# One softmax kernel, one core: 5 of every 64 exponentials move from ScalarE to VectorE

## What is computed

```python
proj = quant4(x) @ ternary_weight(Wqkv_w).T + Wqkv_b      # one projection serves as q, k and v
q = proj.reshape(B, N, h, dk).transpose(0, 2, 1, 3)       # 16 heads of 16
k = v = proj.reshape(B, h, N, dk)
q, k = rotary(q, N), rotary(k, N)
att = einsum('bhnr,bhmr->bhnm', q @ U, k @ U) / sqrt(dk)
y = softmax(att) @ v
x = layernorm(x + quant4(y) @ ternary_weight(Wo_w).T)
x = layernorm(x + ffn(x))         # ternary weights: 256 -> 1024 gated, 1024 -> 1024 twice, -> 256
```

## Time and profile before

| | |
|---|---|
| median of 3 runs | 2773.14 us (2770.94 to 2775.63) |
| the profiled execution: its own time | 2776.77 us |
| its span | 2774.9 us |
| mean granted TensorE clock | 0.978 |
| PE, ACT, DVE, POOL busy | 2511.7, 2093.3, 643.5, 313.9 us |

### The profile page before, as it was taken

How to read it: one execution, slowest core, us unless ns; L and a number is a source line. 1 busy time by engine, 2 the same in 40 slices (tenths; PEclk the granted TensorE clock), 3 DMA queues, 4 the chain that set the end, 5 groups by cost and what they waited for, 6 DMA issues and landing times.

```text
span 2774.9 us, 39861 instructions
## 1 busy us (share of the span) xinstructions
PE 2511.7 (91%) x15898; PEld 1040.0 (37%) x15898; DVE 643.5 (23%) x1241; ACT 2093.3 (75%) x2317; POOL 313.9 (11%) x317
## 2 busy tenths in 40 slices
PE   2678899999999999999999999999977999999998
PEld 1222222222222222222222222222216888888887
DVE  6565410000000000000000000000005665565653
ACT  0467799999999999999999999999972222222222
POOL 2121249994000000000000000000000000000000
PEclk9789999999999999999999999999988999999999
DMA  2333366664323332333233233323321011100100
GB/s 80 99 91 105 98 139 145 153 145 100 66 56 72 66 63 57 66 71 64 59 66 66 58 70 66 66 55 66 68 40 33 1 23 23 23 11 12 23 8 17
DMA packets 101196, 179.56 MB, mean 65 GB/s; under 512 B 31344, under 2 KB 56976, under 8 KB 101024
## 3 DMA queue, kind: packets, MB, share of 16 engines
q1 hardware_dynamic: 91168, 154.16, 26.4%
q0 software_dynamic: 9856, 23.07, 3.5%
HBM read 151.68 MB, written 25.49 MB: 64 GB/s over the span
## 4 chain that ended last, share of the span: by engine, by line
ACT 32%; issue 31%; PE 31%; DVE 5%; ACTq 1%; DMA 0%; SPq 0%; DVEq 0%
ACT PB L572 32%; PE PS L829 17%; PE PS L814 4%; PE PS L280 2%; PE PS L841 2%; PE PS L271 2%; DVE xq L442 1%; PE PS L410 1%; ACTq L570 1%; PE PS L406 1%; DVE xq L479 0%; DVE TD L458 0%; DVE mx L438 0%; DVE V L484 0%; PE PS L795 0%
## 5 line engine op out<-in xcount | busy, mean ns | idle before, releaser
L572 ACT ACTIVATE PB<-PS 128x1024 f32<-128x1024 f32 x2048 | 1884.6, 1219 | 79.0 <-PE PS L271 77.7
L280 PE MATMUL PS<-PB,V 128*17 128x512 f32 x8192 | 1085.8, 602 | 0.5 <-ACT PB L572 0.3
L271 PE MATMUL PS<-QSL,KSL 49*128 49x512 f32 x4096 | 754.1, 446 | 118.0 <-DMA KSL<-KSD 3.9
L271 PEld LDWEIGHTS PS<-QSL,KSL 49*128 49x128 f32 x4096 | 307.0, 186 | 1062.1 <-ACT PB L572 1041.1
L593 DVE STREAM_TRANSPOSE accS<-PS 128x512 f32<-128x512 f32 x32 | 22.9, 716 | 1660.7 <-PE PS L280 1660.7
L904 ACT ACTIVATE hfr<-PS,s 128x512 f32<-128x512 f32 x128 | 86.8, 689 | 300.5 <-PE PS L829 300.4
L280 PEld LDWEIGHTS PS<-PB,V 128*17 128x17 f32 x8192 | 136.1, 95 | 374.7 <-issue 360.2
L829 PE MATMUL PS<-hidden_ar,wh1r 128*128 128x512 f32 x1024 | 237.5, 391 | 0.0
L829 PE MATMUL PS<-hidden_br,wh2r 128*128 128x512 f32 x1024 | 235.3, 390 | 0.0
L829 PEld LDWEIGHTS PS<-hidden_br,wh2r 128*128 128x128 f32 x1024 | 191.7, 188 | 39.5
L829 PEld LDWEIGHTS PS<-hidden_ar,wh1r 128*128 128x128 f32 x1024 | 190.6, 188 | 40.2 <-DVE hfr L993 0.8
(11 more groups left out here) (131 smaller groups left out, 902.3 us busy)
## 6 DMA issues: line engine op xcount, KB each, us to landing
KSL<-KSD SPq DMA_DIRECT2D x256, 256.0 KB
KSL<-KSD SPq DMA_DIRECT2D x256, 128.0 KB
yq<-in_mlp POOLq DMA_DIRECT2D x44, 256.0 KB, 4.0
QSL<-QSD SPq DMA_DIRECT2D x64, 132.0 KB
KSD<-khl SPq DMA_DIRECT2D x64, 128.0 KB
QSD<-qhl SPq DMA_DIRECT2D x32, 256.0 KB
xg<-in_x SPq DMA_DIRECT2D x8, 512.0 KB, 7.2
QSL<-QSD SPq DMA_DIRECT2D x64, 64.0 KB
```

What stands on the lines that cost most here:

```text
L271: ins = pe.matmul(PS[:, 2 * (pair % SLOTS) + e, :], KSL[r, q % 2, s, k * P:(k + 1) * P], QSL[r, b % 2, s, :], start=True, stop=True, tile_ ...
L280: ins = pe.matmul(ACC[i * VW:i * VW + DK + 1, :], V17[:, HT * h + u, c, :], PB[:, (2 * unit + i // 2) % RING, (i % 2) * QW:(i % 2 + 1) * Q ...
L572: act.activation(PB[:, pair % RING, :], PS[:, slot:slot + 2, :].rearrange("p a b -> p (a b)"), ACT.Exp).then_inc(at["probs_ready"], 1)
```

## The change

Five units of a block, numbers 1, 7, 13, 19 and 25, in blocks 8 to 30 (115 units in all), are called late. Their odd pair is no longer exponentiated by ScalarE: VectorE does it with ten instructions of its own on 128 x 1024 elements. It scales the scores by log2(e), splits them into a whole and a fractional part, forms the power of the whole part by a shift, evaluates a polynomial of degree 5 for the fraction, and multiplies. The results go to tiles of their own (`late_act` for the even pair, two of them in turn; `late_dve` for the odd one), and TensorE takes the value sums of a late unit six units later, at unit 7, 13, 19, 25 or 31. Unit 1 has then no sums, and unit 31 has two units' sums. A late unit uses no tile of the ring.

TensorE's step of a late unit waits for `poly_read`, which VectorE's first instruction raises when it has read the scores. VectorE takes the exponential of unit u in its program order at unit u, ahead of `block_dve` for unit 31.

The new tiles lie where the weights `wh2` go later. So the 16 loads of `wh2` leave GpSimd's loop; GpSimd issues them in the last block, one per unit, after the last late sums.

```diff
+LATE_AT, LATE_BLOCKS, LATE_BY = (1, 7, 13, 19, 25), range(8, NB_ALL - 1), 6
+LATE = [KT * _b + _u for _b in LATE_BLOCKS for _u in LATE_AT]
+LATE_NUMBER = {_u: _k for _k, _u in enumerate(LATE)}
+LATE_PAIR = {2 * _u + 1: _k for _k, _u in enumerate(LATE)}
+SUMS_OF = {_u: ([_u - LATE_BY] if _u - LATE_BY in LATE_NUMBER else []) + ([] if _u in LATE_NUMBER else [_u])
+           for _u in range(NB_ALL * KT)}
+TO_WHOLE = ROUND + 127.0
...
         def first_pe(pe, at):
...
-                pe.wait_ge(at["probs_ready"], 2 * unit + 2)
+                for pair in (2 * unit, 2 * unit + 1):
+                    if pair in LATE_PAIR:
+                        pe.wait_ge(poly_read, LATE_PAIR[pair] + 1)
+                    elif pair % 2 or pair + 1 in LATE_PAIR:
+                        pe.wait_ge(at["probs_ready"], BY_ACT[pair])
                 for pair in (2 * unit + 3, 2 * unit + 4):
                     if pair < 2 * units:
                         scores_pe(pe, at, 0, pair)
...
-                sums_pe(pe, at, unit, unit // KT % NBLK)
+                for n in SUMS_OF[unit]:
+                    if n in LATE_NUMBER:
+                        pe.wait_ge(poly_ready, LATE_NUMBER[n] + 1)
+                    first_sums_pe(pe, at, n, unit // KT % NBLK)
...
+        def exponentials_dve(v, s, at, pair):
+            k = LATE_PAIR[pair]
+            slot = 2 * (pair % SLOTS)
+            v.wait_ge(at["scores_ready"], pair + 1)
+            v.tensor_scalar(ey, PS[:, slot:slot + 2, :].rearrange("p a b -> p (a b)"), LOG2E, -126.0, ALU.mult,
+                            ALU.max).then_inc(poly_read, 1)
+            v.wait_ge(poly_read, k + 1)
+            s.did(v.tensor_scalar(et, ey, 127.0, TO_WHOLE, ALU.min, ALU.add))
+            s.settle()
+            s.did(v.scalar_tensor_tensor(ee, et, TO_WHOLE, ey, ALU.subtract, ALU.subtract))
+            s.settle()
+            s.did(v.tensor_scalar(ey, ee, POW2[5], POW2[4], ALU.mult, ALU.add))
+            s.did(v.tensor_scalar(et.bitcast(I32), et.bitcast(I32), 23, None, ALU.logical_shift_left))
+            s.settle()
+            s.did(v.tensor_tensor(ey, ey, ee, ALU.mult))
+            s.settle()
+            for c in (3, 2, 1):
+                s.did(v.scalar_tensor_tensor(ey, ey, POW2[c], ee, ALU.add, ALU.mult))
+                s.settle()
+            if k:
+                v.wait_ge(late_free, k)
+            v.scalar_tensor_tensor(late_dve, ey, POW2[0], et, ALU.add, ALU.mult).then_inc(poly_ready, 1)
+            v.wait_ge(poly_ready, k + 1)
...
         def first_dve(v, s, at):
...
+                if unit in LATE_NUMBER:
+                    exponentials_dve(v, e, at, 2 * unit + 1)
                 if unit % KT == KT - 1:
                     block_dve(v, at, unit // KT)
...
-                pool.dma_start(piece, a["mlp"][:, n * QW:(n + 1) * QW]).then_inc(ready, 16)
+                if ready is not w_in[True][2]:
+                    pool.dma_start(piece, a["mlp"][:, n * QW:(n + 1) * QW]).then_inc(ready, 16)
...
+            pool.wait_ge(late_free, len(LATE))
+            unit = KT * (NB_ALL - 1)
+            for n in range(WCHUNKS):
+                piece, ready = weight_piece(True, n)
+                if ready is w_in[True][2]:
+                    unit += 1
+                    pool.wait_ge(first["probs_free"], IN_RING[unit])
+                    pool.dma_start(piece, a["mlp"][:, n * QW:(n + 1) * QW]).then_inc(ready, 16)
```

More of the change, by code:

```diff
@@ L1 @@
+import itertools
 from contextlib import ExitStack
@@ L71 @@
 SETUP_UNITS = max(SETUP_AT) + 4
+LATE_AT, LATE_BLOCKS, LATE_BY = (1, 7, 13, 19, 25), range(8, NB_ALL - 1), 6
[4 more added lines that the diff above has]
+           for _u in range(NB_ALL * KT)}
+IN_RING = list(itertools.accumulate((int(_u not in LATE_NUMBER) for _u in range(NB_ALL * KT)), initial=0))
+BY_ACT = list(itertools.accumulate(int(_p not in LATE_PAIR) for _p in range(2 * NB_ALL * KT)))
+POW2 = (1.0000001192092896, -0.6931469440460205, 0.24022120237350464, -0.05550713092088699, 0.009675541892647743,
+        -0.001327647129073739)
+LOG2E = 1.4426950408889634
+TO_WHOLE = ROUND + 127.0
 KEYS_AT, CONSTS_AT = {1: 26, 2: 57, 3: 86}, {1: 29, 2: 60, 3: 89}
@@ L148, in postln_block @@
         with ExitStack() as life:
+            _, EXP = scope(("below_EXP", [P, (2 * DC + HC) * HID], F32), ("EXP", [P, 6, 2 * QW], F32))
+            late_act, late_dve, ey, et, ee = [EXP[:, k, :] for k in range(2)], EXP[:, 2, :], EXP[:, 3, :], EXP[:, 4, :], EXP[:, 5, :]
             weights = weight_tiles(life, True)
@@ L202, in postln_block @@
         stored = sem("stored")
+        poly_read, poly_ready, late_free, dve_e = sem("poly_read"), sem("poly_ready"), sem("late_free"), sem("dve_e")
         def attempt(tag, rows):
@@ L548, in load_x, with first_sums_pe @@
             sp.dma_start(xg[:, g % 2, :, :], x_rows[:, g * TQ:(g + 1) * TQ, :]).then_inc(x_in[g % 2], 16)
+        def first_sums_pe(pe, at, unit, hb):
+            kt = unit % KT
+            c, u = divmod(kt, HT)
+            for i in range(BL):
+                h = hb * BL + i
+                if unit in LATE_NUMBER:
+                    probs = late_dve if i >= 2 else late_act[LATE_NUMBER[unit] % 2]
+                else:
+                    probs = PB[:, (2 * IN_RING[unit] + i // 2) % RING, :]
+                ins = pe.matmul(ACC[i * VW:i * VW + DK + 1, :], V17[:, HT * h + u, c, :],
+                                probs[:, (i % 2) * QW:(i % 2 + 1) * QW],
+                                start=kt == 0, stop=kt == KT - 1, tile_position=(0, i * VW))
+            ins.then_inc(late_free if unit in LATE_NUMBER else at["probs_free"], 1)
         def first_pe(pe, at):
@@ L563, in first_pe @@
                     pe.wait_ge(at["acc_saved"], unit // KT + 1)
-                sums_pe(pe, at, unit, unit // KT % NBLK)
+                for n in SUMS_OF[unit]:
+                    if n in LATE_NUMBER:
+                        pe.wait_ge(poly_ready, LATE_NUMBER[n] + 1)
+                    first_sums_pe(pe, at, n, unit // KT % NBLK)
         def first_act(act, at):
             for pair in range(2 * NB_ALL * KT):
-                act.wait_ge(at["scores_ready"], pair + 1)
-                if pair >= RING:
-                    act.wait_ge(at["probs_free"], (pair - RING) // 2 + 1)
@@ L571, in first_act @@
-                slot = 2 * (pair % SLOTS)
-                act.activation(PB[:, pair % RING, :], PS[:, slot:slot + 2, :].rearrange("p a b -> p (a b)"),
-                               ACT.Exp).then_inc(at["probs_ready"], 1)
+                unit, s = divmod(pair, 2)
+                probs = None
+                if pair in LATE_PAIR:
+                    pass
+                elif unit in LATE_NUMBER:
+                    if LATE_NUMBER[unit] >= 2:
+                        act.wait_ge(late_free, LATE_NUMBER[unit] - 1)
+                    probs = late_act[LATE_NUMBER[unit] % 2]
+                else:
+                    n = 2 * IN_RING[unit] + s
+                    if n >= RING:
+                        act.wait_ge(at["probs_free"], (n - RING) // 2 + 1)
+                    probs = PB[:, n % RING, :]
@@ L575, in first_act @@
+                if probs is not None:
+                    act.wait_ge(at["scores_ready"], pair + 1)
+                    slot = 2 * (pair % SLOTS)
+                    act.activation(probs, PS[:, slot:slot + 2, :].rearrange("p a b -> p (a b)"),
+                                   ACT.Exp).then_inc(at["probs_ready"], 1)
                 if pair % 2 and (pair - 5) // 2 in SETUP_AT:
                     setup_act(act, *SETUP_AT[(pair - 5) // 2])
+        def exponentials_dve(v, s, at, pair):
+            k = LATE_PAIR[pair]
+            slot = 2 * (pair % SLOTS)
+            v.wait_ge(at["scores_ready"], pair + 1)
[18 more added lines that the diff above has]
+            v.wait_ge(poly_ready, k + 1)
@@ L578, in first_dve @@
         def first_dve(v, s, at):
-            for unit in range(SETUP_UNITS):
+            e = Steps(v, dve_e)
+            for unit in range(NB_ALL * KT):
                 if unit in SETUP_AT:
                     setup_dve(v, s, *SETUP_AT[unit])
+                if unit in LATE_NUMBER:
+                    exponentials_dve(v, e, at, 2 * unit + 1)
                 if unit % KT == KT - 1:
                     block_dve(v, at, unit // KT)
-            for b in range(SETUP_UNITS // KT, NB_ALL):
-                block_dve(v, at, b)
@@ L589, in block_dve @@
             s = Steps(v, at["dve_step"], 2 * b)
-            v.wait_ge(at["probs_free"], b * KT + KT)
+            v.wait_ge(at["probs_free"], IN_RING[KT * b + KT])
             if b > 0:
```

## The result

The changed kernel takes 2830.84 us (median of 4 runs, 2825.84 to 2832.18) against 2773.21. The ratio is 1.0204, with a 95% interval of 1.0187 to 1.0222: 57.6 us slower. It was forecast as 23.4 slower, 2796.5. The direction and the range held; the size is off by more than a factor of two.

A forecast was written before the change was run, and what follows sets the result against it. ScalarE bounds the kernel; after the change waits set a block at 43.5 + 10.79 + 5.40 = 59.69 us against 58.66, +23.7 over 23 blocks, +23.4 with edges: 2773.1 + 23.4 = 2796.5, range 2778 to 2846.

The forecast's parts named there:

- What bounds, and that the shares mislead: Attention blocks: ScalarE sets the pace at 58.66 us; busy shares promise 4.6 us a block, but waits between engines decide.
- VectorE's durations: VectorE's exponential: seven instructions of 1.224 us and three of 0.69, the shift's 0.69 being assumed without a row.
- its slow end: VectorE's int32 shift at one element per clock, 1.22 us: chain 11.41, +49 us, 2845; 9 in 100.
- The interval: Six units between two late units take 10.88 us against 11.00 now; four such intervals a block, 43.5 us.
- the chain: VectorE's ten dependent instructions for one late exponential, 10.88 us, taken to set the interval between late units.
- the floor: Shortest interval with a free VectorE: ScalarE's nine exponentials, then VectorE's read before TensorE's next scores, 10.78 us.
- The block's end: Step 31 to the next block's step 1: double sums, block_dve, then unit 1's read, 5.40 us against 3.67, +1.73.
- The clock: TensorE falling to half clock, put with keys coming late as a rival: above 2850, 5 in 100.
- So little changes: Clock argument: TensorE's steps fill 52.8 us of a 59.7 us block, where now it has them in 58.7.
- TensorE would be seen waiting for VectorE 115 times: Sign of being right: TensorE's L271 waits for VectorE's new tensor_scalar about 115 times.
- The faster rival: ScalarE never drains and stays the bound: six units 10.09 us, block 56.6, -48 us, 2725; 7 in 100.

The follow-up runs named there:

- e4: Changed kernel with polynomial degree 3 and TensorE waiting for VectorE's read only before the second pair of scores: 2759.48 us, 0.9937 of the kernel before.
- e6: Changed kernel with four late units (3, 10, 17, 24), sums seven units later, wait only before the second pair of scores, degree 5: 2758.13 us.
- e8: Changed kernel with three late units (3, 12, 21), sums nine later, the last's in four parts, wait only before the pair needing the slot: 2754.95 us.
- e3: Changed kernel with TensorE waiting for VectorE's read only before the second of the two pairs of scores: 2792.75 us, 1.0059 of the kernel before.
- e2: Changed kernel with two middle polynomial steps left out, degree 3 in place of 5: 2833.18 us, 1.0202 of the kernel before.
- e9: Changed kernel with four late units (1, 8, 15, 22), sums seven later, unit 22's in four parts, wait only before the second pair: 2754.87 us.
- e5: Changed kernel without late unit 1, leaving 7, 13, 19 and 25: 2787.09 us, 1.0052 of the kernel before.
- e1: Changed kernel without VectorE's exponential: ScalarE takes all pairs, only the late units' sums move: 2790.38 us, 1.0052 of the kernel before.
- e7: Changed kernel plus eight idle TensorE products at the end of step 0 and in step 1 of blocks 8 to 30: 2809.76 us.

## Why the prediction was right and wrong

- **What bounds, and that the shares mislead: right.** The 4.6 us a block that the busy shares promised were never there. Even with the waits mended little of it comes in: 0.70 of 4.6 with five units (e4), 0.73 of 3.7 with four (e6), 0.95 of 2.8 with three and the sums spread (e8).
- **VectorE's durations: right to 0.01 us.** Seven at 1.22, three at 0.69, the shift among them (0.685). The Trainium skill's rule for tensor_scalar on fp32 ("VectorE: DVE Perf Modes", "The perf-mode tier table (the rule you actually need)"), carried over to the shift, had left its slow end out; the trace agrees with it, and the range had reached to 2846 for that case.
- **The interval: right mechanism, first mis-sized term.** Forecast 10.88, measured 10.99. I took the chain as the longer of the two (10.88 against a floor of 10.78). The chain was right: its terms add up to 10.87, not 10.88, and e3 measures 10.87; the floor was 0.21 too low, so it is the floor that holds, as e2 shows, at 10.99. Its handovers were too cheap: 0.54 taken from the scores to their reader (the rows give 132.27 - 131.74 = 0.53), measured 0.62 for VectorE and 0.59 for ScalarE; and 0.06 taken for TensorE's restart, read off a transpose, measured 0.15 (766.16 to 766.31). Where only the second pair of scores waits for the read, the restart takes 0.05 (e9, 1234.45 to 1234.50); why it differs is open. Against the forecast that is 0.11 in each of four intervals.
- **The block's end: right.** 5.40 forecast, 5.48 measured, and 10.79 against 10.83 before it (777.14 - 766.31). e5 confirms the read's part by taking it away, -1.09, and e1 measures the other, the double sums, at 0.61, together 1.70 where the term had 1.73. Together the waits cost 36.8 us instead of 23.7; 13 of the 34 us missed.
- **The clock: the step that failed.** "So little changes" compared TensorE's mean load over a block, 52.8 in 59.7 against 52.8 in 58.7 us. The clock fell behind the hole: 3.78 busy in 5.90 us, though no gap in it is over 0.95, then 1.2 GHz for 3.4 us, 18 times. It cost 18.4 us, the largest part of the 34 missed, and my sum had it at nothing; e7 shows the cause. I had given it 5 in 100 and only in a severe form. The early window that I quoted already mixed both levels at 87% busy; the reading to make was where within it they changed.
- **TensorE would be seen waiting for VectorE 115 times: wrong as a reading,** 23 by the table; e2 and e3, not the table, show that the others wait as well.
- **The faster rival** ("ScalarE never drained") is refuted in a stronger form than I gave: e4 and e6 took away the read and the chain, and it still drained. That more slots would cure it is argued and not tested.

The remaining 2 us between the medians' difference and that of the spans are within what runs differ by. Why 5 of the 23 blocks kept the full clock with the same instructions stays open; the drift of the dip from block to block says that its place in the hole matters.

## What to carry to other kernels

Relieving the busiest engine of some instructions saves only what its neighbours let it run ahead: count the slots between them, and follow step by step who sets the pace behind a moved instruction. Here two steps were shorter, by 0.18 and 0.15, and then the old pace was back: 0.33 us saved of 0.92. When a second reader takes over a buffer, let each producer step wait only for the slot that it overwrites, and don't put the new reader behind other work at a boundary. And for TensorE's clock look at the emptiest stretch, not at the mean: a hole with 2.1 us of idleness cost another 1.0 through the clock, and filling it with idle products won that back.

## What the hardware showed unexpectedly

- TensorE's granted clock fell to its lower level for 3.4 us after a stretch of 5.9 us in which it was 64% busy, and not after the same stretch in 5 other blocks. A dip costs 1.02 us at these loads. In e2 it lasted 6.8 us three times and 10.2 once, at a cost of 2.4 and 3.7.
- 16 products of constants a block, 2.1 us of added TensorE work, made the kernel 21 us faster, 18 of it by keeping that clock.
- An int32 shift of 128x1024 in SBUF takes 0.685 us, as fast as an fp32 tensor_scalar with constants.
- TensorE restarts with scores 0.15 us after VectorE's read ends when both pairs wait for it, 0.05 when only the second does (e9), and with sums 0.05 after the transpose.
